# A recommendation kernel's start-up: layer 2's weight copy, the splits and the gathers moved, and transposes of the unit matrix added on TensorE

## What is computed

```python
inputs = emb[feature_ids] * feature_vals[:, :, None]          # (B, 39, 16)
h = inputs
for i in range(3):                                            # 200 outputs each
    x = einsum('bhd,bmd->bhmd', h, inputs).reshape(B, -1, 16)
    x = relu(einsum('bcd,oc->bod', x, Ws[i]) + bs[i][None, :, None])
    h, direct = (x[:, :100], x[:, 100:]) if i != 2 else (None, x)
    finals.append(direct)
cin = sum(concatenate(finals, axis=1), axis=-1)
d = relu(relu(inputs.reshape(B, -1) @ dnn_W0.T + dnn_b0) @ dnn_W1.T + dnn_b1)
out = concatenate((cin, d), axis=1) @ fc_W.T + fc_b + sum of the biases
```

## Time and profile before

| | us |
|---|---|
| median of 3 runs | 2751.63 |
| lowest and highest | 2749.88, 2753.76 |
| the profiled execution | 2752.34 |
| its span | 2750.5 |
| PE busy in the span | 2649.5 (96%) |
| DVE, POOL, ACT busy | 2285.0, 2249.6, 1834.6 |
| mean granted TensorE clock | 0.992 of full |

### The profile page before, as it was taken

One profiled execution on the slowest core, in us unless ns is written; L12 is line 12 of the kernel. 1 busy time (PEld: TensorE's weight loads), 2 busy tenths in 40 slices (PEclk: granted clock), 3 DMA queues, 4 the chain that ended last, 5 costly groups with the idle time before them and its releaser, 6 DMA issues.

```text
span 2750.5 us, 66670 instructions
## 1 busy us (share of the span) xinstructions
PE 2649.5 (96%) x17928; PEld 2640.2 (96%) x17928; DVE 2285.0 (83%) x4584; ACT 1834.6 (67%) x4776; POOL 2249.6 (82%) x1912
## 2 busy tenths in 40 slices
PE   0699999999999999999999999999999999999999
PEld 0599999999999999999999999999999999999998
DVE  2788888888888888888888888888888888888884
ACT  0576776766767667676777767677677766766663
POOL 6788888888888888888888888888888888877763
PEclk9799999999999999999999999999999999999999
DMA  8844545445444454544545455454554545545441
GB/s 149 199 124 123 133 126 130 124 118 144 116 133 125 118 149 112 136 121 122 146 111 138 120 131 137 114 136 118 138 131 118 133 117 140 129 117 136 111 115 51
DMA packets 199914, 349.82 MB, mean 127 GB/s; under 512 B 66632, under 2 KB 118697, under 8 KB 199615
## 3 DMA queue, kind: packets, MB, share of 16 engines
q1 hardware_dynamic: 185782, 342.81, 45.6%
q0 software_dynamic: 10496, 2.88, 3.1%
q10 hardware_dynamic: 3464, 2.68, 0.3%
HBM read 344.29 MB, written 14.17 MB: 130 GB/s over the span
## 4 chain that ended last, share of the span: by engine, by line
PE 94%; POOL 2%; SPq 2%; DVE 1%; issue 1%; DMA 1%; ACT 0%; POOLq 0%; ACTq 0%; DVEq 0%
PE acc L642 61%; PE acc L643 28%; PE acc L667 2%; POOL raw L498 1%; PE hrep L678 1%; DVE W L1061 0%; SPq L319 0%; DMA odd<-lin 0%; PE acc L742 0%; PE acc L743 0%; PE acc L744 0%; SPq L309 0%; DMA raw<-table,idx 0%; PE hrep L764 0%; PE hrep L766 0%
## 5 line engine op out<-in xcount | busy, mean ns | idle before, releaser
L642 PE MATMUL acc<-W,xhi_d 128*128 128x400 f32 x5632 | 1732.4, 367 | 17.2 <-DVE xlo_d L1087 10.6
L643 PE MATMUL acc<-W,xlo_d 128*128 128x200 f32 x5632 | 1434.9, 255 | 0.0
L1087 DVE TENSOR_TENSOR xlo_d<-prod_d,xhi_d 128x512 fp32r<-128x512 f32 (+1 forms) x1536 | 983.9, 641 | 205.1 <-ACT xhi_d L819 147.2
L1079 DVE TENSOR_TENSOR prod_d<-hrep,xrep 128x512 f32<-128x512 f32 (+1 forms) x1536 | 1039.0, 677 | 105.8 <-issue 27.7
L548 POOL TENSOR_TENSOR xlo_p<-prod_p,xhi_p 128x512 fp32r<-128x512 f32 (+1 forms) x768 | 953.8, 1242 | 181.3 <-ACT xhi_p L813 135.6
L642 PEld LDWEIGHTS acc<-W,xhi_d 128*128 128x128 f32 x5632 | 1059.9, 188 | 20.1 <-DVE xlo_d L1087 12.9
L643 PEld LDWEIGHTS acc<-W,xlo_d 128*128 128x128 f32 x5632 | 1078.4, 191 | 0.0
L819 ACT ACTIVATE xhi_d<-prod_d 128x512 fp32r<-128x512 f32 (+1 forms) x1536 | 885.1, 577 | 222.6 <-PE acc L643 199.8
L642 PE MATMUL acc<-W,xhi_p 128*128 128x400 f32 x2944 | 917.2, 363 | 12.9 <-POOL xlo_p L548 12.9
L542 POOL TENSOR_TENSOR prod_p<-hrep_s,xrep 128x512 f32<-128x512 f32 x512 | 665.9, 1301 | 161.3 <-ACT hrep_s L856 108.5
L643 PE MATMUL acc<-W,xlo_p 128*128 128x200 f32 x2944 | 751.7, 255 | 0.0
(11 more groups left out here) (92 smaller groups left out, 927.1 us busy)
## 6 DMA issues: line engine op xcount, KB each, us to landing
xrep<-xs SPq DMA_DIRECT2D x384, 384.0 KB
l0x<-xs SPq DMA_DIRECT2D x378, 136.5 KB
xrep<-xs SPq DMA_DIRECT2D x384, 128.0 KB
xrep<-xs SPq DMA_DIRECT2D x128, 336.0 KB
xrep<-xs SPq DMA_DIRECT2D x128, 64.0 KB
l0x<-xs SPq DMA_DIRECT2D x378, 19.5 KB
lin<-w SPq DMA_DIRECT2D x8, 750.0 KB
raw<-table,idx POOLq DMA_INDIRECT x328
```

The source lines that it names most:

```text
L642: pe.matmul(bank[:, 0:2 * OUTS], hi, w, start=first, stop=last, skip_group_check=True)
L643: return pe.matmul(bank[:, 0:OUTS], lo, w[:, 0:OUTS], start=False, stop=last, skip_group_check=True)
L1079: nc.vector.tensor_tensor(to, h, xrep[:, (par + layer - 1) % 2, a:a + count, :], ALU.mult).then_inc(s_prod_d, 1)
L1087: op = nc.vector.tensor_tensor(xlo_d[:, slot, 0:split], bank[:, 0:split], xhi_d[:, slot, 0:split].bitcast(F32), ALU.subtract)
```

## The change

Layer 2's copy goes from SP to ACT: three quarters behind the first three splits of layer 1, the fourth behind the other two. ACT's splits of layer 1 stand ahead of high(-1, P0) and behind high(-1, P1). SP issues load_layer0(2) and layer 2's load ahead of chunk 1's blocks. In step 1 the splits of layer 2 follow D0 to D4 in place of D4 to D8, and POOL makes the low part of the piece (0, 8), with a semaphore of its own. POOL issues no gathers ahead of step 1's last product; then four, and four in each of steps 2 to 9, three in step 10. The scaling of a tile, the turn and the stores of its inputs come one step later in the loop. PE gets 110 transposes of the unit matrix ahead of first_inputs, 40 behind it and 30 ahead of turn(0, 0). Cut to its core:

```diff
-        W2_AT = {4: 0, 5: 1, 6: 2, 7: 3, 8: 4}
+        W2_AT = {0: 0, 1: 1, 2: 2, 3: 3, 4: 4}
...
@@ sync
             for e in (1, 2, 0, 3):
                 load_block(0, 0, e)
-            rows_of_weights(sp, 2, w2)
-            sp.wait_ge(s_pt, 4)
             sp.wait_ge(s_prod_p, p_num(0, 1) + 1)
             load_layer0(2)
+            load_weights(sp, 2, w2)
+            sp.wait_ge(s_pt, 4)
             for e in (1, 2, 0, 3):
                 sp.wait_ge(s_xblk[e], BLOCK_SEM[e])
                 load_block(1, 1, e)
-            load_weights(sp, 2, w2)
...
@@ gpsimd
-            pool.wait_ge(s_xin, 3)
-            gather(0)
             product(-1, 1, 0)
...
+            pool.wait_ge(s_xin, 3)
+            product(1, 1, 1)
+            low(1, 0)
+            product(1, 1, 2)
+            low(1, 1)
+            a, b = PIECES[2][1]
+            pool.wait_ge(s_whi, W_DONE[1] + 2)
+            nc.gpsimd.tensor_tensor(weights(2)[:, a:b, 1, :], raw_weights(2, a, b),
+                                    weights(2)[:, a:b, 0, :].bitcast(F32), ALU.subtract).then_inc(s_wlo2, 1)
+            product(1, 1, 3)
+            low(1, 2)
+            product(1, 1, 4)
+            low(1, 3)
+            product(1, 1, 5)
+            low(1, 4)
+            for m in range(FIRST[0]):
                 gather(m)
+            product(2, 0, 0)
+            low(1, 5)
...
@@ tensor
+            def turn_nothing(times):
+                for _ in range(times):
+                    pe.transpose(hrep[1][:, 0, :], ident[:], ident[:])
...
+            pe.wait_ge(s_wlo, W_DONE[0])
+            turn_nothing(110)
             first_inputs(0, (prod_d[0], prod_d[1]))
             first_inputs(1, (prod_d[2], acc[2]))
+            turn_nothing(40)
             multiply(-1, "P", 0)
             multiply(-1, "P", 1)
+            turn_nothing(30)
             turn(0, 0, -1)
...
@@ scalar
             split_weights(0, 0)
+            for n in range(3):
+                split_weights(1, n)
+            rows_of_weights(act, 2, w2, range(3))
             high(-1, "P", 0)
             high(-1, "P", 1)
+            split_weights(1, 3)
+            split_weights(1, 4)
+            rows_of_weights(act, 2, w2, (3,))
             high(0, "P", 0)
-            split_weights(1, 0)
-            split_weights(1, 1)
+            high(0, "P", 1)
             low_copy(0, 0, -1)
...
@@ vector
-                    if isinstance(i, int) and i == 1 and d in W2_AT:
+                    if isinstance(i, int) and i == 1 and W2_AT.get(d, 1) != 1:
                         split_weights(2, [W2_AT[d]])
...
-            split_weights(1, [0, 1])
+            split_weights(1, [0])
             dve.wait_ge(s_fc, 32)
             evacuate(0, 0)
-            split_weights(1, [2])
+            split_weights(1, [1, 2])
             product(0, 0, 0)
             product(0, 0, 1)
+            split_weights(1, [3])
```

More of the change, by code:

```diff
@@ L209, in rec_kernel @@
         s_wlo = sem("weights_low")
+        s_wlo2 = sem("second_piece_of_w2_low")
         s_ident = sem("ident_set")
@@ L289, in spread_of @@
             return (0, CHUNKS + 1) if isinstance(i, int) and i == CHUNKS else (layer - 1, i + 2 - layer)
-        W2_AT = {4: 0, 5: 1, 6: 2, 7: 3, 8: 4}
-        W_NEEDED = [{("P", 0): 1},
-                    {("D", 0): 2, ("P", 2): 3, ("D", 2): 4, ("D", 4): 5, ("D", 5): 6},
-                    {("D", 6): 7, ("P", 4): 8, ("D", 8): 9, ("D", 10): 10, ("D", 11): 11}]
+        W2_AT = {0: 0, 1: 1, 2: 2, 3: 3, 4: 4}
+        W_NEEDED = [{("P", 0): (s_wlo, 1)},
+                    {("D", 0): (s_wlo, 2), ("P", 2): (s_wlo, 3), ("D", 2): (s_wlo, 4), ("D", 4): (s_wlo, 5),
+                     ("D", 5): (s_wlo, 6)},
+                    {("D", 6): (s_wlo, 7), ("P", 4): (s_wlo2, 1), ("D", 8): (s_wlo, 8), ("D", 10): (s_wlo, 9),
+                     ("D", 11): (s_wlo, 10)}]
         def pairs(c):
@@ L299, in pairs, with rows_of_weights @@
                 :, c * L0_SLOTS * L0_ROWS:(c + 1) * L0_SLOTS * L0_ROWS].rearrange("p (s r) -> p s r", r=L0_ROWS)
-        def rows_of_weights(engine, layer, src):
+        def rows_of_weights(engine, layer, src, quarters):
             used = H_QUARTER * FIELDS
             full = used // QUARTER
-            for q in range(4):
+            for q in quarters:
                 rows = lin[layer][used * q:used * (q + 1), :]
@@ L341, in _ @@
             sp.dma_start(val[:], vals.rearrange("(p t) m -> p (t m)", p=P)).then_inc(s_small, 16)
-            rows_of_weights(sp, 1, w1)
+            rows_of_weights(sp, 1, w1, range(4))
             sp.dma_start(fcw[:], fc_w.partition_broadcast(P)).then_inc(s_fc, 16)
@@ L449, in _ @@
                 for j in range(DIM):
-                    if j == 10:
+                    if j == 11:
                         store_inputs(k + 1)
-                    if j == 11:
+                    if j == 12:
                         store_dense_inputs(k + 1)
@@ L552, in p_groups, with step @@
                 return [g for kind, g in step_order(i) if kind == "P"]
-            def step(i, par, ahead, rows=()):
+            def step(i, par, ahead):
                 mine = p_groups(i)
                 for at, k in enumerate(mine):
-                    for m in rows[at * len(rows) // len(mine):(at + 1) * len(rows) // len(mine)]:
-                        gather(m)
                     if at + 1 < len(mine):
@@ L564, in step @@
                     low(i, k)
-            FREE_AT = 8
+            FREE_AT = 9
             COUNTS = [2] * 5 + [3] * 9 + [2]
-            BEFORE = sum(COUNTS[0:DIM - 1 - FREE_AT])
+            FIRST = [4 * n + 4 for n in range(FREE_AT)] + [FIELDS]
             def gathers(j):
@@ L595, in _ @@
             low(0, 1)
-            for m in range(1, 4):
-                gather(m)
             product(0, 0, 2)
@@ L600, in _, with tile_step, first_gathers @@
             low(0, 2)
-            for m in range(4, 7):
-                gather(m)
             product(1, 1, 0)
             low(0, 3)
-            for m in range(7, 9):
-                gather(m)
-            step(1, 1, 0, range(9, BEFORE))
-            with pool.Fori(0, TILES - 1) as k:
-                for j in range(DIM):
[L610 to L614, removed]
+            pool.wait_ge(s_xin, 3)
[14 more added lines that the diff above has]
+            for m in range(FIRST[0]):
+                gather(m)
+            product(2, 0, 0)
+            low(1, 5)
+            def tile_step(k, j, rows):
+                rows(j)
+                if j == FREE_AT:
+                    scale(k + 1, True)
+                    copy_idx((k + 2) % TILES, k + 2)
+                step(k * DIM + (j + 2), j % 2, 0)
+            def first_gathers(j):
+                if j < FREE_AT:
+                    for m in range(FIRST[j], FIRST[j + 1]):
+                        gather(m)
+                else:
+                    gathers(j)
+            for j in range(DIM):
+                tile_step(0, j, first_gathers)
+            with pool.Fori(1, TILES - 1) as k:
+                for j in range(DIM):
+                    tile_step(k, j, gathers)
             for i in range(2 + DIM * (TILES - 1), CHUNKS):
@@ L660, in multiply @@
                 if isinstance(i, int) and c == 0 and (kind, g) in W_NEEDED[layer]:
-                    pe.wait_ge(s_wlo, W_NEEDED[layer][(kind, g)])
+                    pe.wait_ge(*W_NEEDED[layer][(kind, g)])
                 for n, t in enumerate(tiles):
@@ L1050, in split_weights @@
                     a, b = PIECES[layer][n]
-                    done = W_DONE[layer] - len(PIECES[layer]) + n + 1
-                    dve.wait_ge(s_whi, done)
+                    dve.wait_ge(s_whi, W_DONE[layer] - len(PIECES[layer]) + n + 1)
                     src, hi, lo = raw_weights(layer, a, b), weights(layer)[:, a:b, 0, :], weights(layer)[:, a:b, 1, :]
```

9 lines of the change are left out of this document (2 added, 7 removed).

## The result

| | before | after |
|---|---|---|
| median, us (11 runs each) | 2749.88 | 2757.69 |
| lowest to highest | 2748.54 to 2756.7 | 2756.26 to 2762.26 |
| the profiled execution, and its span | 2752.34, 2750.5 | 2756.46, 2754.6 |

The ratio of all runs is 1.0024, 95% interval 1.0015 to 1.0033: slower by 0.24% (the two medians of the table alone give 0.28%). The same code before, timed again beside the experiments (28, 23, 11 and 19 runs), had medians of 2751.73, 2751.95, 2752.44 and 2753.62, so that the change costs 4 to 8 us, most likely about 6. The two profiled executions are 4.1 us apart.

What follows compares the result with a forecast made beforehand. TensorE was taken as full from 200 us, so the end moves with P0 of step 2: 115 + 28.4 + 6 = 149.4, +6.8 us, 2759.1 on the profiled execution, 0.7 less for the median: 2758.4, range 2749.5 to 2765.

Steps and rivals of the forecast that it cites:

- POOL's queue: POOL's work from P2 of step 1 to P0 of step 2: products, low parts, weights piece and eight gathers, 28.4 us.
- The sum: P0 of step 2 moves from 142.65 to 115 + 28.4 + 6 = 149.4, so +6.8 us.
- Layer 1's weights and ACT: At the start: weights land at 64, copy's third quarter sticks to about 80, ACT's first high part at 79.
- the mark: Prediction: start of P0 of step 2 on PE, 142.65 before; after measuring: first weight load of step 3's P0.
- The load's start: SP starts layer 2's load at 89 instead of 90.46, with blocks and copy through at 86.5 again.
- P2 of step 1: POOL's product waits for chunk 1's block 0, issued behind the load: 112 to 118, taken at 115, against 106.71.
- the high bound: Each of chunk 1's blocks waits for the engines of the load's tail, so block 0 lands at 118.
- DVE locked out: 6 us: In step 1, DVE's low parts of layer 2 wait under POOL's unbroken run: 0 to 9 us, taken at 6.
- The 110 transposes: 0 to 1.4 us late: Ahead of first_inputs: they start at 49 and end at 62.3 to 64, against first_inputs at 62.58.
- Their clock: On PE, transposes alone raise the clock from 1.2 to 2.4 GHz; starts stand 0.21 us apart slow, 0.11 fast.
- Four gathers to a step: In steps 2 to 9, POOL has 19.6 us of work in a step of 20.18, so it fits.
- Rival (a): DVE finds its gaps and blocks land early: P2 at 112 to 114, time 2749.4 to 2754.4; chance 0.25.

Runs made afterwards that it cites:

- the copy into idle transfers: Changed kernel without transposes, eight gathers early, ACT issuing layer 2's whole copy once tile 0's rows are gathered, load directly behind chunk 0's blocks: 2759.51 us (1.0028).
- the last experiment: All 180 transposes put back into the kernel with layer 2's load last, its splits and POOL's piece later, and the whole copy early on ACT: 2746.98 us (0.9978).
- the one without its transposes: Changed kernel without transposes, whole copy early on ACT, layer 2's load last, its splits behind D5 to D9, POOL's piece later, gathers early: 2744.32 us (0.9974).

## Why the prediction came out as it did

The forecast was 2758.4, the time is 2757.69, and the sign and the engine (POOL's queue into step 2) were right. That the number fits so well is in part luck. The sum put P0 of step 2 at 149.4, 6.8 us later; the profile has it at 144.50, 1.85 us later, and below the 146 to 153 that the prediction named as a sign of being right. Three more of its signs did not come: no low part took 5 to 12 us, ACT's first high part was at 72.86 and not at 75 to 81, and PE was not slow again when multiply(-1) began.

- **Layer 1's weights and ACT.** Forecast: landing at 64, the third quarter's issue stuck to 80, the first high part at 79. In the changed kernel's profile the weights landed at 62.9, the copy was issued before the blocks, its third quarter stuck for only 2.52 us, and the high part came at 72.86. In the kernel without transposes it stuck to 77.0, and the high part came at 77.07. The step describes one of the orders that occur. With a landing by 63.5 (three kernels) the copy came before the blocks. With a later one it met them: at 65.7 and 66.6 the third quarter stuck for 7.64 and 6.98 us, but with the four gathers early, also at 65.7, only the fourth did (7.47 us) and the high part came at 71.11. It did not matter to the mark.
- **The load's start.** Forecast 89, measured 84.32, and 79.6 to 87.8 in the four others with this copy and this order of transfers. This step failed: chunk 0's blocks and the copy were not through at 86.5 but by about 84, since the copy used 64 to 68, which had been nearly empty.
- **P2 of step 1.** Forecast 115 (112 to 118), measured 111.82, and 112.4 to 114.7 in four others with the same order of transfers. The value taken, 115, was 3.2 us too late in the profile, and that 112 is near is luck: the load's last issue came at 96.2 and not at 104, and P2 15.6 us behind it, where the two bounds had 8 and 14. The DMA engines were full until 109 (share 1.03 to 1.15), so the blocks had to wait for their share of the engines, as in the high bound and longer.
- **POOL's queue.** Forecast 28.4 us, measured 32.5. The items were all there; the term was mis-sized because each was priced as if alone. Four of them met a piece of DVE: 2.57 for a low part of 1.00, 2.88 for a product of 1.28, 2.05 for 1.26 and 1.90 for 1.29, together 4.6 us.
- **DVE locked out: 6 us.** This failed for the changed kernel: no piece lasted over 3 us. The premise that POOL keeps its turn while its next instruction is ready does not hold always: at 119.16 POOL's next product was ready, and DVE's piece of 118.19 ran first. POOL paid instead, by the term above. That the mechanism exists is shown by the 9.73 us of the copy into idle transfers and the 8.97 us of the last experiment. What decides between the two is not known: the last experiment and the one without its transposes have the same order of work and show 8.97 and 2.90.
- **The 110 transposes: 0 to 1.4 us late.** Measured 6.3 us late in the changed kernel's profile and 4.5 in that of the last experiment. Where they began at 47.9 or later they took 13.7 to 15.1 us, which agrees with the forecast. What failed is the case of holes, which the trace of before could not show. The 10 us of idle PE behind the 40 did not come either: multiply(-1) began at 75.33, right behind them, at full clock. That all this is worth nothing at the end held (2758.42 without them).
- **Their clock.** The 40 behind first_inputs took 4.53 us, 0.11 each, and from 66 to 68, with nothing but the 110 on PE, the granted clock was 1.00. The Trainium skill, page "TensorE: Matmul & The Clock Gate", section "Part 4: PE-mode transpose", says that the clock does not engage for them; the trace does not agree.
- **Four gathers to a step** fit, as forecast: from the mark on the steps take 20.18 or 20.19 us each.
- **Left out:** the 3.74 us of idle PE ahead of P0 and the half clock behind it, 1.5 us. The prediction priced a stall at its length alone.

So P2 forecast 3.2 us too late and DVE's 6 us too much stand against POOL's 4.1 and the clock's 1.5 too little. In the profiled execution the sum is off by 2.6 us (2759.1 forecast, 2756.46 measured); that the medians agree to 0.7 comes on top, as that execution was 1.2 us under its median. Rival (a) describes the trace better than the forecast does: its conditions (P2 before 114, no low part over 3 us) and its mark (140.4 to 145.4) were met. Its time (2749.4 to 2754.4) was not. It too left out the 1.5 us of half clock, and only its up to 3 us of waits made room for the 4.1 us that were missing in the 28.4. The rest between 3.54 us at the mark and about 6 in the medians is not settled. A part of it is that the profiled execution of the changed kernel had an early P2 (111.82 against a mean of 112.9 over this and those four), and that of before was 2.5 us above its median.

## What to carry to other kernels

When two engines exclude each other, price the stretch on both: what one gains by not being locked out, the other pays, so a queue's length is not the sum of what its items take alone. Which of the two pays can differ between profiles of the same order of work, so give it as a range. Before reordering transfers against each other, look for a stretch in which few run (59 to 67 us here, share 0.21 before), and let the work that needs the last ones stand last in every engine's queue. And of a queue that sets the end, first move out what could run in its idle time before: eight gathers brought the whole change back to level.

## What the runs showed of the hardware

- **A lock-out can last a whole run of instructions.** One DVE subtraction of 1600 columns took 1.82 to 1.83 us alone. Asked for during POOL's own piece, it took 2.2 to 2.9 us in seven kernels and 3.61 in one, with POOL's next product stretched to up to 2.9; in two others POOL went on and it took 9.73 and 8.97. POOL had a next instruction ready in all ten. The Trainium skill, page "SBUF — State Buffer", section "Terms", calls the port pair that DVE and GpSimd share exclusive and held for the full instruction. The traces agree that one waits, but in these two the wait went over six of POOL's instructions and not one.
- **A run of equal transposes can stop midway.** The 110 transposes stopped behind the 42nd and took 5 to 8 us over the next two or three, in both kernels where they began before 47.5. In the six that began at 47.9 to 51.0 they took 13.7 to 15.1 us. The DMA engines do not tell the two apart: their share was 1.10 from 53 to 56 in the changed kernel, and 1.08 to 1.12 from 50 to 56 in the six. The cause is open.
- **The same pause costs 2 or 4 us.** Each profile has one pause of POOL in the loop (6.0 to 6.8 us, "issue", near 600 us), and PE waits 1.5 to 2.3 us for it. In six the clock stays up and the steps around lose 1.9 to 2.6 us, in seven it falls to half behind the pause and they lose 3.8 to 4.2, in kernels with and without the change (before: 2.3; after: 3.8). A row of the changed kernel's list of waits names it (us in all, times, longest):

```profile
PE acc L667 <- POOL xlo_p L551: 1.9, 1, 1.9
```
